# Fused feed-forward, scan and feed-forward kernel: the normalised rows become f16 operands by DMA transposes instead of TensorE f32 transposes

## The chip, the cores and the metric

The kernel runs on one core of a Trainium2 chip. The metric is the device time of one execution in microseconds (us), and the median of the runs counts. Engines are named as in the profile: PE is TensorE, DVE is VectorE, ACT is ScalarE, POOL is GpSimd, SP is SyncE, which here only issues DMAs. "SPq" is SP's queue of DMA issues.

## What is computed

A block of three residual steps on 4096 rows (2 x 2048 tokens) of 1024 channels. The first and the third step are the same routed feed-forward, the second is a selective scan over the tokens.

```
x = x + 0.5 * ffn(layernorm(x), A, B, W, bias)
x = x + scan(layernorm(x), W_xproj, W_dt, b_dt, A_log, D)
x = x + 0.5 * ffn(layernorm(x), A, B, W, bias)

def ffn(x, A, B, W, bias):
    vecs   = einsum('arh,bsh->bsar', A, x)            # 64 experts of rank 16
    routes = top 4 of 64 by norm(vecs), each 1/4
    v      = einsum('bsa,bsar->bsr', routes, vecs)
    delta  = einsum('bsa,ajr,bsr->bsj', routes, B, v)
    return einsum('bsh,jh->bsj', x, W) + bias + delta

def scan(x, ...):
    h = exp(delta * A) * h + delta * B_t * x          # 16 states a channel
    y = sum(h * C_t) ; return y + x * D
```

## The kernel before

Work is cut into 64 units of 128 rows: 32 of the first feed-forward (kind 1) and 32 of the second (kind 2), in an order that `plan` fixes. Units 3 to 60 carry the scan along: its 1024 steps (64 tiles of 16 steps, four groups of four steps a tile) are spread evenly, about 18 a unit. Every engine has a program written out in order, with semaphores between them; nothing is reordered at run time. `scans`, `decays`, `loads` and `states` with two numbers mean "the scan's work between these twentieths of the unit".

In unit *a* the next unit is called *b*. PE does for *a* the product with W (`base`), the scan's small products, the product with B (`routed`), and at the end of the unit already the product of *b* with A (`experts`), each in two halves (nb) of three thirds. The products are f16 in two parts: an operand is a high part plus a low part, `xT[:, 0]` and `xT[:, 1]`, each 128 channels by 128 rows times 8. Thirds 0 and 1 read the high part, third 2 reads the low part. So PE needs the whole of `xT[:, 0]` for *b* at the first of `experts`, and the low part at third 2.

Before the change the operand of *b* is made thus. DVE takes the row statistics (`unit_stats`), ACT works out scale and shift (`prepare`) and writes the normalised rows in f32 to `xn` (`normed`, L842). PE turns them in eight f32 transposes of 128 x 128 into two PSUM banks (`norm_blocks`, L552 with `xn`). ACT copies each bank to `xT[:, 0]` as f16 (`high`, L847), and DVE subtracts that from the bank to give `xT[:, 1]` (`low_part`, L1094). `xn` is used a second time, for the rows that feed the scan (L867), and a third, for its small projections.

SP's order in a unit is: the load of the next rows (L342), the store of the scan's input (L448), two DMA transposes of `uT`, the operand of `routed` (L409), then the scan's loads of twentieths 2 to 9, two small stores (L455, L456), the scan's loads of twentieths 9 to 18, the load of y (L336) and the store of the result (L468). The scan's loads are spreads of 512 KB from scratch memory to all partitions (L361 for POOL's inputs, L354 for ACT's decays), a tile's store (L400) and its second load (L396), and at a new chunk of rows spreads of B and C (L367, L373). POOL's products with B and C are L512, L518 and L528, DVE's scan is L1157, ACT's decays are L942.

Of the kernel before, what the change touches and what calls it, by code (L numbers as in the profile page):

```python
# [119 lines left out]
def build(nc, x, AT, BT, WT, bias, WxT, WdtT, b_dt, A_log, D_par, out):  # L120
# [41 lines left out]
    with ctx:  # L162
# [43 lines left out]
        pjs = xn[:, 0:NX]  # L206
        drs = auxs[:, 0:P]
# [55 lines left out]
        s_xT = sem("s_xT"); s_xhi = sem("s_xhi"); s_xlo = sem("s_xlo")  # L263
        s_vec = sem("s_vec"); s_sq = sem("s_sq"); s_n2 = sem("s_n2"); s_mk = sem("s_mk"); s_gm = sem("s_gm")
# [38 lines left out]
        def _(sp):  # L303
# [106 lines left out]

            def loads(a, lo, hi):
# [28 lines left out]
            def unit(l, a, b):  # L440
# [22 lines left out]
                loads(a, 9, 18)  # L463
# [83 lines left out]
        def _(pe):  # L547
# [20 lines left out]
            def norm_blocks(b, half):  # L568
                if half == 0:
                    pe.wait_ge(s_xn, b.u + 1)  # L570
                if half == 0:
                    pe.wait_ge(s_u, b.u * 2)
                blocks(ptn[half], lambda k: xn[:, (half * KB + k) * P:(half * KB + k + 1) * P], s_xT, idf[:, :])
# [32 lines left out]
            def first_base(a):  # L606
# [10 lines left out]
                for k in range(KD):  # L617
                    pe.wait_ge(s_loW, k + 1)
                    for nb in range(2):
                        nc.tensor.matmul(po[:, nb, :], xT[:, 0, k, :], wW[:, 1, k, nb * HF:(nb + 1) * HF],  # L620
                                         start=False, stop=False)

            def experts(b, nb, third):
                if nb == 0 and third != 1:
                    pe.wait_ge(s_xhi, b.u * 2 + 2)
                    pe.wait_ge(s_xlo, b.u * 2 + (1 if third == 0 else 2))
                last = product(pv[:, nb, :], xT, wA, nb, third, True, True)
                if third == 2:
                    last.then_inc(s_vec, 1)

            def base(a, nb, third):
# [7 lines left out]
                product(po[:, nb, :], xT, wW, nb, third, False, False)  # L639
# [92 lines left out]
            def unit(l, a, b):  # L732
# [61 lines left out]
            norm_blocks(US[0], 0)  # L794
            norm_blocks(US[0], 1)
# [5 lines left out]
        def _(act):  # L801
# [37 lines left out]
            def normed(b, nT):  # L839
# [5 lines left out]
            def high(b, half):  # L845
                act.wait_ge(s_xT, b.u * 2 + 1 + half)
                nc.scalar.activation(xT[:, 0, half * KB:(half + 1) * KB, :].rearrange("p k t -> p (k t)"), ptn[half],  # L847
                                     ACT.Copy).then_inc(s_xhi, 1)
# [16 lines left out]
            def normed2(a, xT_done):  # L865
                act.wait_ge(s_xT, xT_done)
# [78 lines left out]
            def unit(l, a, b):  # L945
# [37 lines left out]
                if b:  # L983
                    normed(b, 2 * (a.f1s - (a.kind == 1)))
                decays(10, 12)
                if b:
                    high(b, 0)
                if b:
                    high(b, 1)
# [15 lines left out]
                if a.kind == 1:  # L1005
                    normed2(a, a.u * 2 + 4)
# [4 lines left out]
            normed(US[0], 0)  # L1011
            high(US[0], 0)
            high(US[0], 1)
# [15 lines left out]
        def _(dve):  # L1029
# [52 lines left out]
            def unit_stats(b):  # L1082
# [4 lines left out]
                dve.wait_ge(s_xn, b.u)  # L1087
                stats("ln1", xin[:, b.p, :], s_mv)

            def low_part(b, half):  # L1090
                dve.wait_ge(s_xhi, b.u * 2 + 1 + half)
                hi = xT[:, 0, half * KB:(half + 1) * KB, :].rearrange("p k t -> p (k t)")
                lo = xT[:, 1, half * KB:(half + 1) * KB, :].rearrange("p k t -> p (k t)")
                V.tensor_tensor(lo, ptn[half], hi, ALU.subtract).then_inc(s_xlo, 1)  # L1094

# [156 lines left out]
            low_part(US[0], 0)  # L1252
            low_part(US[0], 1)
# [56 lines left out]
```

## Time and profile before

| what | value |
|---|---|
| median of 3 runs | 2722.13 us (2721.1 to 2724.64) |
| profiled execution | 2721.68 us, span 2719.8 us |
| PE busy | 2593.5 us, 95% of the span |
| POOL busy | 2350.0 us, 86% |
| DVE busy | 2227.7 us, 82% |
| ACT busy | 1505.0 us, 55% |
| DMA engines | q1, the queue of SP's issues, 43.8% of 16 engines |
| granted PE clock | 0.987 of full speed |

The span is what the profile covers of the execution; 1.9 us lie around it. POOL has nothing to do in the scan's absence, at the start and at the end, so its share is that of a stretch and not of the whole.

### The profile page before, as it was taken

The page shows a single profiled execution, that of the slowest core. Times are in us where ns is not written, and L with a number is a line of the kernel's source. Part 1 is how long each engine was busy: PE and PEld are TensorE (multiplying, and loading weights), DVE is VectorE, ACT ScalarE, POOL GpSimd, SP SyncE. Part 2 cuts the span into 40 slices and gives each one's busy share as a digit, 9 for nine tenths or more (in the row PEclk, how much of TensorE's full clock was granted, in tenths as well). Part 3 has the DMA queues.
Part 4 walks back from the last instruction along what each step waited for, and adds up shares of the span by engine and source line. Part 5 has one row for each costly group of instructions (what it writes and reads, how often), then busy time and mean ns, then how long its engine had stood idle before and what let it go on. Part 6 is the DMA issues. An engine that isn't in the chain of part 4 may idle for free.

```text
span 2719.8 us, 39965 instructions
## 1 busy us (share of the span) xinstructions
PE 2593.5 (95%) x13664; PEld 1178.2 (43%) x13664; DVE 2227.7 (82%) x2933; ACT 1505.0 (55%) x3363; POOL 2350.0 (86%) x703
## 2 busy tenths in 40 slices
PE   4989999999989999999999999999999999999999
PEld 1444444444434444444444444444444444444444
DVE  8448888888878898888888988888888889989943
ACT  5347666665545555555556555555555555656521
POOL 2138998899999999999998999999999999999910
PEclk8989999999999999999999999999999999999999
DMA  5145444644464454645454455544555455554321
GB/s 223 52 117 154 144 148 135 172 141 144 131 183 150 136 156 130 190 141 147 139 177 139 147 153 156 157 130 147 156 172 149 134 156 161 159 144 150 103 63 54
DMA packets 333217, 390.29 MB, mean 143 GB/s; under 512 B 149459, under 2 KB 249939, under 8 KB 333014
## 3 DMA queue, kind: packets, MB, share of 16 engines
q1 hardware_dynamic: 316118, 354.18, 43.8%
q10 hardware_dynamic: 16896, 33.56, 4.0%
q8 instruction: 108, 1.77, 0.3%
q14 instruction: 95, 0.78, 0.1%
HBM read 250.82 MB, written 103.29 MB: 130 GB/s over the span
## 4 chain that ended last, share of the span: by engine, by line
PE 57%; DVE 16%; POOL 6%; DMA 6%; issue 5%; ACT 4%; DVEq 4%; ACTq 1%; SPq 0%; POOLq 0%
PE po L560 20%; PE pv L560 9%; PE po L564 9%; DVE mreg L1157 7%; PE py L727 6%; PE pv L564 4%; POOL mreg L518 3%; PE pv L689 2%; POOL mreg L528 2%; DMA delta_scratch<-mreg 2%; DVE sel L1114 2%; PE pv L708 1%; PE pv L552 1%; DVEq L1116 1%; DMA uT<-sel 1%
## 5 line engine op out<-in xcount | busy, mean ns | idle before, releaser
L528 POOL TENSOR_TENSOR mreg<-mreg 128x2048 f32<-128x2048 f32 x256 | 1163.0, 4543 | 70.7 <-ACT hst L928 70.0
L1157 DVE TENSOR_TENSOR_SCAN mreg<-pA,hst,mreg 128x512 f32<-128x512 f32 (+1 forms) x1024 | 1048.9, 1065 | 50.2 <-ACT pA L942 43.8
L942 ACT ACTIVATE pA<-mreg,nA 128x512 f32<-128x512 f32 (+1 forms) x1280 | 744.4, 598 | 410.0 <-DVE mreg L1157 379.4
L518 POOL TENSOR_TENSOR mreg<-mreg 128x1024 f32<-128x1024 f32 x340 | 796.4, 2370 | 118.3 <-DMA mreg<-delta_scratch 103.8
L560 PE MATMUL po<-wB,uT 128*128 128x512 f16 x2016 | 471.0, 382 | 12.1 <-DVE xin L1080 7.5
L560 PE MATMUL po<-wW,xT 128*128 128x512 f16 x2016 | 474.5, 382 | 0.0
L560 PE MATMUL pv<-wA,xT 128*128 128x512 f16 x2016 | 461.1, 381 | 8.3 <-ACT mreg L911 7.2
L512 POOL TENSOR_TENSOR mreg<-mreg 128x2048 f32<-128x2048 f32 x86 | 390.2, 4537 | 4.0 <-issue 3.8
L560 PEld LDWEIGHTS pv<-wA,xT 128*128 128x128 f16 x2016 | 191.5, 98 | 284.5 <-issue 51.7
L560 PEld LDWEIGHTS po<-wB,uT 128*128 128x128 f16 x2016 | 193.4, 98 | 266.0 <-issue 48.3
L560 PEld LDWEIGHTS po<-wW,xT 128*128 128x128 f16 x2016 | 196.4, 99 | 250.2 <-issue 40.6
L727 PE MATMUL py<-mreg,Em 128*32 128x512 f32 (+1 forms) x2560 | 273.9, 518 | 6.3 <-DVE mreg L1168 6.1
L1157 DVE TENSOR_TENSOR_SCAN mreg<-pA,cst,mreg 128x256 f32<-128x256 f32 (+1 forms) x256 | 244.0, 997 | 15.7 <-ACT pA L942 14.1
L564 PE MATMUL po<-wB,uT 128*128 128x512 f16 x1008 | 238.4, 379 | 0.0
L564 PE MATMUL po<-wW,xT 128*128 128x512 f16 x1008 | 238.4, 379 | 0.0
L564 PE MATMUL pv<-wA,xT 128*128 128x512 f16 x1008 | 238.3, 379 | 0.0
L1098 DVE TENSOR_REDUCE n<-sel 128x32 f32<-128x512 f32 x128 | 87.5, 684 | 172.5 <-ACT sel L855 172.2
L1130 DVE SCALAR_TENSOR_TENSOR xin<-po,sc,xin 128x512 f32<-128x512 f32 x128 | 94.1, 735 | 85.6 <-PE po L564 82.0
L564 PEld LDWEIGHTS po<-wW,xT 128*128 128x128 f16 x1008 | 96.3, 98 | 132.8 <-issue 20.5
L564 PEld LDWEIGHTS pv<-wA,xT 128*128 128x128 f16 x1008 | 97.5, 98 | 125.7 <-issue 10.0
L564 PEld LDWEIGHTS po<-wB,uT 128*128 128x128 f16 x1008 | 96.2, 98 | 122.9 <-issue 21.3
L1071 DVE BATCH_NORM_STATS2 ln_st<-xin 128x6 f32<-128x512 f32 x192 | 122.7, 681 | 9.2 <-DMA xin<-x 3.0
(132 smaller groups left out, 2357.6 us busy)
## 6 DMA issues: line engine op xcount, KB each, us to landing
mreg<-delta_scratch SPq DMA_DIRECT2D x256, 512.0 KB, 5.1
mreg<-xnT_scratch SPq DMA_DIRECT2D x128, 256.0 KB, 5.2
delta_scratch<-mreg ACTq DMA_DIRECT2D x128, 256.0 KB
xin<-x SPq DMA_DIRECT2D x32, 512.0 KB, 4.7
x_scratch<-xin SPq DMA_DIRECT2D x32, 512.0 KB, 4.7
xnT_scratch<-auxs SPq DMA_DIRECT2D x32, 512.0 KB, 3.2
yT_scratch<-mreg SPq DMA_DIRECT2D x64, 256.0 KB, 4.9
uT<-yT_scratch SPq DMA_DIRECT2D x32, 512.0 KB, 6.1
```

Of the source, the lines that this page charges most:

```text
L512: pool.tensor_tensor(h, u, b.broadcast_to([P, 4 * c.parts, c.width]), ALU.mult).then_inc(s_bm, 2)
L518: pool.tensor_tensor(h[:, half * n:half * n + n, :], u, b.broadcast_to([P, n, c.width]), ALU.mult).then_inc(s_bm, 1)
L528: pool.tensor_tensor(h, h, by_c, ALU.mult).then_inc(s_cm, 1)
L560: last = nc.tensor.matmul(dst, lhs[:, 0, k, :], w[:, wb, k, nb * HF:(nb + 1) * HF], start=(first and k == 0 and wb == 0), stop=False)
L564: last = nc.tensor.matmul(dst, lhs[:, 1, k, :], w[:, 0, k, nb * HF:(nb + 1) * HF], start=False, stop=(stop and k == KD - 1))
L689: last = nc.tensor.matmul(pj[:, 0:NX], auxs3[:, k, :], wx[:, k, :], start=(k == 0), stop=(k == KD - 1))
L727: last = nc.tensor.matmul(split(py[32 * s:32 * s + 32, :], c)[:, n, :], Em[:, :], h[:, c.parts * s + n, :], start=(g == 0 and n == 0), sto ...
L942: last = nc.scalar.activation(dst[:, part, :], src[:, part, :], ACT.Exp, scale=nA[:, m:m + 1])
L1071: V.bn_stats(t["st"][:, 6 * n:6 * n + 6], src[:, n * HF:(n + 1) * HF])
L1098: V.tensor_reduce(n2[:, nb * NE // 2:(nb + 1) * NE // 2], sel3[:, nb * NE // 2:(nb + 1) * NE // 2, :], AX.X, ALU.add)
L1130: V.scalar_tensor_tensor(dst, po[:, nb, :], sc[:, 3:4], dst, ALU.mult, ALU.add).then_inc(s_res, 1)
L1157: last = V.tensor_tensor_scan(h, split(pA[:, i % 2, :], c)[:, part, :], h, before, ALU.mult, ALU.add)
```

## The change

The transposes of the normalised rows go from PE to the DMA engines, for units 1 to 63 (unit 0 keeps the old way).

- ACT writes the rows at once as f16 in row form (`high_rows`, into the first half of `xn`'s memory, now called `xr`), in the place of the f32 write. A step later it writes the same rows in f32 to the two PSUM banks (`full_rows`, 512 channels each), in the place of the two copies, one step of `decays` earlier.
- DVE subtracts the f16 rows from the banks and writes the low part in row form (`low_part`), in its old place.
- SP issues two DMA transposes of 256 KB each (`turn_rows`): that of the high part between the two small stores and the loads of twentieth 9, that of the low part between the loads of twentieths 9 to 11 and those from 11 on. The first waits for `high_rows` (and for `base` to be done with the old operand), the second for both halves of `low_part`.
- PE loses `norm_blocks` and waits at `experts` for the landing of these two instead.
- The statistics, and the second small step of a tile on DVE (`delta` at position 1), stay where they are.

```diff
+            def turn_rows(b, part):
+                if part == 0:
+                    sp.wait_ge(s_bs, b.u)
+                    sp.wait_ge(s_xhi, b.u + 2)
+                else:
+                    sp.wait_ge(s_xlo, b.u * 2 + 2)
+                sp.dma_start_transpose(xT[:, part, :, :], xr[:, part, :]).then_inc(s_xc[part], 16)
...
-                loads(a, 9, 18)
+                if b:
+                    turn_rows(b, 0)
+                loads(a, 9, 11)
+                if b:
+                    turn_rows(b, 1)
+                loads(a, 11, 18)
...
             def experts(b, nb, third):
                 if nb == 0 and third != 1:
-                    pe.wait_ge(s_xhi, b.u * 2 + 2)
-                    pe.wait_ge(s_xlo, b.u * 2 + (1 if third == 0 else 2))
+                    pe.wait_ge(s_xc[third // 2], 16 * b.u)
+                    pe.wait_ge(s_xlo, b.u * 2 + 1)
...
                 routed(a, 1, 1)
-                if b:
-                    norm_blocks(b, 0)
-                if b:
-                    norm_blocks(b, 1)
                 states(a, 10)
...
+            def high_rows(b, nT):
                 act.wait_ge(s_nT, nT)
                 act.wait_ge(s_pq, nT // 2)
-                nc.scalar.activation(xn[:, :], xin[:, b.p, :], ACT.Identity, scale=lnb["ln1"]["r"][:, :],
-                                     bias=lnb["ln1"]["nm"][:, :]).then_inc(s_xn, 1)
+                act.wait_ge(s_xc[0], 16 * (b.u - 1))
+                act.wait_ge(s_xc[1], 16 * (b.u - 1))
+                nc.scalar.activation(xr[:, 0, :], xin[:, b.p, :], ACT.Identity, scale=lnb["ln1"]["r"][:, :],
+                                     bias=lnb["ln1"]["nm"][:, :]).then_inc(s_xhi, 1)
+            def full_rows(b, half):
+                act.wait_ge(s_u, b.u * 2)
+                nc.scalar.activation(ptn[half], xin[:, b.p, half * HF:(half + 1) * HF], ACT.Identity,
+                                     scale=lnb["ln1"]["r"][:, :], bias=lnb["ln1"]["nm"][:, :]).then_inc(s_xn, 1)
...
             def low_part(b, half):
+                dve.wait_ge(s_xn, b.u * 2 + 1 + half)
+                dve.wait_ge(s_xhi, b.u + 2)
+                dve.wait_ge(s_xc[1], 16 * (b.u - 1))
+                cols = slice(half * HF, (half + 1) * HF)
+                V.tensor_tensor(xr[:, 1, cols], ptn[half], xr[:, 0, cols], ALU.subtract).then_inc(s_xlo, 1)
```

On SP, in unit 37 of the kernel before, the scan's loads stand around the two small stores (L455, L456) like this; L361 and L354 are spreads, L400 a tile's store.

```order
L361 DMA mreg<-delta_scratch 128x1x1024 [waits s_bm,s_std] x2
L400 DMA yT_scratch<-mreg 128x4x128 [waits s_y]
L354 DMA mreg<-delta_scratch 128x1x1024 [waits s_dA,s_std]
L455 DMA delta_rank_scratch<-auxs 128x128 [waits s_pc]
L456 DMA bc_scratch<-auxs 32x128
L354 DMA mreg<-delta_scratch 128x1x1024 [waits s_dA,s_std]
L396 DMA mreg<-xnT_scratch 128x4x128 [waits s_sty]
```

The same place of the change (its line numbers are some lines on: L363 is the old L361, L356 the old L354, L402 the old L400).

```order
L363 DMA mreg<-delta_scratch 128x1x1024 [waits s_bm,s_std] x2
L402 DMA yT_scratch<-mreg 128x4x128 [waits s_y]
L356 DMA mreg<-delta_scratch 128x1x1024 [waits s_dA,s_std]
L465 DMA delta_rank_scratch<-auxs 128x128 [waits s_pc]
L466 DMA bc_scratch<-auxs 32x128
L419 DMA_TRANSPOSE xT<-xn 128x8x128 [waits s_xhi,s_bs]
L419 DMA_TRANSPOSE xT<-xn 128x8x128 [waits s_xlo]
L356 DMA mreg<-delta_scratch 128x1x1024 [waits s_dA,s_std]
L398 DMA mreg<-xnT_scratch 128x4x128 [waits s_sty]
```

Nothing of the old order moved; two transposes with waits of their own stand in front of the second spread of decays. In other units zero to four of the scan's loads stand between the two.

On PE, in the same unit, before the change, from the middle of `routed` to `experts`:

```order
L560 MATMUL po<-wB,uT 128x512 x16
L552 MATMUL pv<-idf,xn 128x128 [waits s_u,s_xn]
L552 MATMUL pv<-idf,xn 128x128 x3
L552 MATMUL pt<-idf,xn 128x128 x4
L564 MATMUL po<-wB,uT 128x512 x8
L727 MATMUL py<-mreg,Em 32x512 [waits s_cm]
L727 MATMUL py<-mreg,Em 32x512 x3
L560 MATMUL pv<-wA,xT 128x512 [waits s_xlo,s_xhi]
L560 MATMUL pv<-wA,xT 128x512 x15
L564 MATMUL pv<-wA,xT 128x512 [waits s_xlo,s_xhi]
```

And in the change (L575 is the old L560, L579 the old L564, L743 the old L727):

```order
L575 MATMUL po<-wB,uT 128x512 x16
L579 MATMUL po<-wB,uT 128x512 x8
L743 MATMUL py<-mreg,Em 32x512 [waits s_cm]
L743 MATMUL py<-mreg,Em 32x512 x3
L575 MATMUL pv<-wA,xT 128x512 [waits s_xlo,s_xc0]
L575 MATMUL pv<-wA,xT 128x512 x15
L579 MATMUL pv<-wA,xT 128x512 [waits s_xlo,s_xc1]
```

The eight transposes are gone, and the two waits at `experts` are now for landings (`s_xc0`, `s_xc1`) instead of for ACT and DVE.

## Rows read from the trace of the kernel before

**Rows 1.** Page, part 1: busy us (share of the span) xinstructions.

```profile
PE 2593.5 (95%) x13664; PEld 1178.2 (43%) x13664; DVE 2227.7 (82%) x2933; ACT 1505.0 (55%) x3363; POOL 2350.0 (86%) x703
```

**Rows 2.** Windows: length, busy us by engine, PE clock, DMA share, GB/s.

```profile
253.00:2533.00 2280.00, 2214.04 (x11746) 997.96 (x11745) 1969.40 (x2531) 1331.48 (x2970) 2204.34 (x647) 0.99 0.51 150
...
1530.00:1730.00 200.00, 196.97 (x1019) 87.82 (x1016) 176.39 (x210) 116.28 (x245) 199.22 (x61) 1.00 0.52 152
430.00:530.00 100.00, 93.20 (x539) 43.91 (x532) 83.79 (x128) 62.38 (x152) 89.24 (x27) 0.97 0.58 163
```

**Rows 3.** Timeline of PE, end of unit 29: start us, us, line, tiles.

```profile
1318.55 0.60 PE L552 MATMUL pv<-idf,xn 128*128 128x128 f32 x4
1318.99 0.60 PE L552 MATMUL pt<-idf,xn 128*128 128x128 f32 x4
1319.42 1.89 PE L564 MATMUL po<-wB,uT 128*128 128x512 f16 x8
...
1322.24 3.63 PE L560 MATMUL pv<-wA,xT 128*128 128x512 f16 x16
1325.71 1.89 PE L564 MATMUL pv<-wA,xT 128*128 128x512 f16 x8
```

**Rows 4.** Timeline of ACT, same stretch.

```profile
1316.37 1.22 ACT L842 ACTIVATE xn<-xin,ln_nm,ln_r 128x1024 f32<-128x1024 f32 x1
...
1319.68 0.59 ACT L847 ACTIVATE xT<-pt 128x512 f16<-128x512 f32 x1
```

**Rows 5.** Timeline of DVE, same stretch.

```profile
1319.82 0.69 DVE L1094 TENSOR_TENSOR xT<-pv,xT 128x512 f16<-128x512 f32 x1 [0.23 <-ACT xT L847]
1320.43 1.27 DVE L1157 TENSOR_TENSOR_SCAN mreg<-pA,hst,mreg 128x512 f32<-128x512 f32 x1
1321.62 0.67 DVE L1094 TENSOR_TENSOR xT<-pt,xT 128x512 f16<-128x512 f32 x1
```

**Rows 6.** Line L409, all: issue ns min/median/max, then its landing times.

```profile
L409 SPq DMA_TRANSPOSE uT<-sel x128: 1231/1274/4571, 65.5 to 2702.8; - x128
...
DMA to landing us min/median/max: 3.0/3.2/8.1
```

**Rows 7.** DMA issues landing late, window 1088 to 1094: KB, us to landing.

```profile
xin<-x SPq DMA_DIRECT2D x1, 512.0 KB, 8.7
xnT_scratch<-auxs SPq DMA_DIRECT2D x1, 512.0 KB, 9.3
...
uT<-sel SPq DMA_TRANSPOSE x1, 8.1
```

**Rows 8.** Timeline of SP's issues in the same stretch.

```profile
1090.78 0.74 SPq L448 DMA_DIRECT2D xnT_scratch<-auxs  x1
1092.89 7.02 SPq L409 DMA_TRANSPOSE uT<-sel  x2
```

**Rows 9.** Timeline of SP, unit 37.

```profile
1648.82 0.52 SPq L354 DMA_DIRECT2D mreg<-delta_scratch  x1
1649.39 1.32 SPq L455 DMA_DIRECT2D delta_rank_scratch<-auxs  x1
1650.76 1.73 SPq L456 DMA_DIRECT2D bc_scratch<-auxs  x1
1658.29 0.52 SPq L354 DMA_DIRECT2D mreg<-delta_scratch  x1
```

**Rows 10.** Landings of the first L354 and of L456 above, window of each.

```profile
DMA to landing us min/median/max: 10.9/10.9/10.9
...
DMA to landing us min/median/max: 10.2/10.2/10.2
```

**Rows 11.** Timelines of ACT and PE, unit 37.

```profile
1652.86 1.23 ACT L842 ACTIVATE xn<-xin,ln_nm,ln_r 128x1024 f32<-128x1024 f32 x1
...
1659.51 3.63 PE L560 MATMUL pv<-wA,xT 128*128 128x512 f16 x16
```

**Rows 12.** Unit 2: SP's last spread, its landing, PE's first product.

```profile
155.43 0.71 SPq L373 DMA_DIRECT2D mreg<-bc_scratch  x1
...
DMA to landing us min/median/max: 9.1/9.1/9.1
...
157.72 3.62 PE L560 MATMUL pv<-wA,xT 128*128 128x512 f16 x16
```

**Rows 13.** Windows around a pause of PE, columns as in Rows 2.

```profile
448.00:451.00 3.00, 0.75 (x6) 0.42 (x4) 2.96 (x4) 2.25 (x7) 3.00 (x2) 1.00 0.36 109
451.00:454.30 3.30, 3.23 (x6) 1.23 (x7) 3.00 (x5) 1.20 (x3) 3.30 (x2) 0.51 0.65 145
```

**Rows 14.** Window around two L409 transposes, columns as in Rows 2.

```profile
1182.10:1185.50 3.40, 3.40 (x21) 1.17 (x19) 3.40 (x4) 1.75 (x4) 3.26 (x2) 1.00 0.81 154
```

**Rows 15.** Timeline of SP, unit 50: two spreads merged into one row.

```profile
2192.59 16.59 SPq L361 DMA_DIRECT2D mreg<-delta_scratch  x2
2209.23 0.59 SPq L400 DMA_DIRECT2D yT_scratch<-mreg  x1
```

**Rows 16.** Waits, whole span: total us, times, longest.

```profile
DVE xT L1094 <- ACT xT L847: 66.3, 49, 4.9
```

More of the change, by code:

```diff
@@ L263, in build @@
         s_xT = sem("s_xT"); s_xhi = sem("s_xhi"); s_xlo = sem("s_xlo")
+        s_xc = [sem(f"s_xc{n}") for n in range(2)]; s_bs = sem("s_bs")
         s_vec = sem("s_vec"); s_sq = sem("s_sq"); s_n2 = sem("s_n2"); s_mk = sem("s_mk"); s_gm = sem("s_gm")
@@ L638, in base @@
                     nc.tensor.matmul(po[:, nb, :], onesb[:, :], brow[:, nb * HF:(nb + 1) * HF], start=True, stop=False)
-                product(po[:, nb, :], xT, wW, nb, third, False, False)
+                last = product(po[:, nb, :], xT, wW, nb, third, False, False)
+                if (nb, third) == (1, 2):
+                    last.then_inc(s_bs, 1)
             def first_routed(a):
@@ L837, in prepare, with first_normed, first_high @@
                 refine("ln1", 1)
-            def normed(b, nT):
+            def first_normed(b):
+                nc.scalar.activation(xn[:, :], xin[:, b.p, :], ACT.Identity, scale=lnb["ln1"]["r"][:, :],
+                                     bias=lnb["ln1"]["nm"][:, :]).then_inc(s_xn, 2)
+            def first_high(half):
+                act.wait_ge(s_xT, 1 + half)
+                nc.scalar.activation(xT[:, 0, half * KB:(half + 1) * KB, :].rearrange("p k t -> p (k t)"), ptn[half],
+                                     ACT.Copy).then_inc(s_xhi, 1)
+            def high_rows(b, nT):
                 act.wait_ge(s_nT, nT)
                 act.wait_ge(s_pq, nT // 2)
-                nc.scalar.activation(xn[:, :], xin[:, b.p, :], ACT.Identity, scale=lnb["ln1"]["r"][:, :],
-                                     bias=lnb["ln1"]["nm"][:, :]).then_inc(s_xn, 1)
[L845 to L848, printed above, removed]
+                act.wait_ge(s_xc[0], 16 * (b.u - 1))
[6 more added lines that the diff above has]
+                                     scale=lnb["ln1"]["r"][:, :], bias=lnb["ln1"]["nm"][:, :]).then_inc(s_xn, 1)
             def squares(b, nb):
@@ L983, in unit @@
                 if b:
-                    normed(b, 2 * (a.f1s - (a.kind == 1)))
-                decays(10, 12)
+                    high_rows(b, 2 * (a.f1s - (a.kind == 1)))
+                decays(10, 11)
                 if b:
-                    high(b, 0)
+                    full_rows(b, 0)
                 if b:
-                    high(b, 1)
+                    full_rows(b, 1)
+                decays(11, 12)
                 magnitudes(a, 1)
@@ L1010, in _ @@
             prepare(US[0])
-            normed(US[0], 0)
-            high(US[0], 0)
-            high(US[0], 1)
+            first_normed(US[0])
+            first_high(0)
+            first_high(1)
             act.wait_ge(s_scl, 1)
```

34 lines of the change are left out of this document (18 added, 16 removed).

## The prediction

> **What bounds the kernel now.** I read the page first: PE is busy 95% of the span and POOL 86% [rows 1]. Since POOL works only in the scan, I then asked for windows. In the 2280 us from 253 to 2533 PE is busy 2214 us and POOL 2204 us, so PE has 66 us idle there and POOL 76 [rows 2]. In the 200 us from 1530 on both are full, PE 197.0 us and POOL 199.2; around 430 to 530 both have holes [rows 2]. So two engines bound the kernel side by side. Work taken from PE alone shortens it at most until POOL is full, and a wait put on PE costs nearly its length, because PE has 0.6 us (3 us over 4.8 units from 1530) to 1.2 us (66 us over 54 units) to spare in a unit of 42.2 us (2280 us over 54 units).
>
> Next, the place of the change, at the end of unit 29. The eight transposes hold PE from 1318.55 to 1319.42 [rows 3], and PE asks for the high operand at 1322.24 and for the low one at 1325.71 [rows 3]. ACT has the normalised rows ready at 1317.59 (1316.37 + 1.22) [rows 4], and DVE ends the low part at 1322.29 (1321.62 + 0.67) [rows 5]. So today the high operand exists 2 us, and the low one 3.4 us, before PE wants it.
>
> **What goes.** PE loses 1319.42 − 1318.55 = 0.87 us a unit [rows 3], in 63 units 54.8 us. (Each row's own 0.60 us overlaps the next; the starts count.) ACT's work is the same in kind and size: one 1024-wide write and two 512-wide ones. DVE's subtraction keeps its size, and its wait for ACT (66.3 us in 49 cases [rows 16]) mostly goes, since the PSUM banks no longer wait for PE. That makes the low part earlier by up to 1.3 us where it waited, and by 0.2 us in unit 29 [rows 5]. DVE is no bound, so I count it only there.
>
> **What comes, undisturbed.** An existing transpose of this very size is issued in 1.27 us and lands 3.2 us (median) after its issue starts, at least 3.0 [rows 6]. High part in unit 29: 1317.6 + 3.2 = 1320.8, wanted at 1322.24 − 0.87 = 1321.4: covered by 0.6 us. Low part: 1322.1 + 3.2 = 1325.3, wanted at 1325.71 − 0.87 = 1324.8: PE waits 0.5 us. So even the undisturbed case has no cover left. I laid these two sums over all 63 units. The high part alone is in time nearly everywhere; the low part is 0.1 to 0.8 us late in about a third of the units, and in time where ACT's wait used to hold it up.
>
> **What comes, behind other transfers.** This decides. The same transposes take up to 8.1 us [rows 6]. At 1090.78 a 512 KB store was issued that landed 9.3 us later, at 1100.1; the transpose issued at 1092.89 landed 8.1 us later, at 1101.0 [rows 7, 8]. In all 128 cases of L409 the landing is about the larger of 3.1 us and "1.1 us after the last earlier issue of SP has landed". The Trainium skill (DMA: Bandwidth & Descriptors, section Queues, rings and completion order) says that each engine takes descriptors in the order of its ring; the rows above agree.
>
> The old transposes of uT stand in a quiet place. The new ones stand among the spreads. Unit 37: a spread issued at 1648.82 lands 10.9 us later, at 1659.7, and the small store of 1650.76 at 1661.0 [rows 9, 10]. Rows are ready at 1654.1 (1652.86 + 1.23) [rows 11]; the high transpose, behind both, lands near 1661 to 1662, while PE wants it at 1659.51 − 0.87 = 1658.6 [rows 11]: 2.3 to 3.5 us of wait. By this rule, unit for unit:
> - units 2 and 3, the first spreads. In unit 2 the last of eight is issued at 155.43 and lands 9.1 us later, at 164.5; plus 1.1 gives 165.6 against 157.72 − 0.87 = 156.9 [rows 12]: 8.8 us. Unit 3 likewise 6.8 us. Together 15.6 us. Unit 0, without cover, 1.8 us.
> - 16 further units wait 1.1 to 4.3 us for the high part (unit 37 counts with 3.4), together 38 us.
> - the low part adds 15 us over some 20 units (0.1 to 2.6 us). If a store and a spread issued between the two transposes take as long as the slowest rows show, it is 56 us instead.
>
> Waits 15.6 + 1.8 + 38 + 15 = 71 us, less 54.8: PE's path grows by 16 us.
>
> **Two additions.** First, gains and losses don't offset fully: where POOL is full (the 1530 window), a unit without a wait can't be shorter, while a wait still lengthens its unit. About half of the 0.87 us in some 12 such units is lost: 5 us. Second, PE's clock: PE was busy 0.75 us of the 3.0 before 451, and the granted clock in the next 3.3 us was 0.51 (1.2 GHz instead of 2.4) [rows 13]; such a stretch costs about 1.7 us of full-speed work. Eight new waits are over 2 us; I count half of them followed by one: 6 us. The sum is 2721.7 (the profiled execution's own time) + 16 + 5 + 6 = 2749; that execution is 0.4 us below the median. I take 2745, a little lower, since waits on PE let the scan's engines run ahead and some waits then meet an already earlier `high_rows`.
>
> **Costed at nothing.** DMA work: two transposes hold 0.81 of the engines for 3.4 us [rows 14], so two more a unit add 2.8 us in 42, at a DMA share of 0.51 [rows 2]. It is covered by free DMA time; uncovered it shows as later spreads. SP's queue: the second transpose waits for DVE, and behind it stand the spreads of twentieths 11 on. In unit 50 the first L361 goes out at 2192.59 and would now go at about 2207.4; but its partner goes only shortly before 2209.2 anyway [rows 15], when POOL frees the buffer, so the pair as a whole is ready as before. In unit 37 the spread of 1658.29 [rows 9] would go at about 1659.7, behind a transpose that can be issued at 1658.4. By the same reckoning something behind is held by 2 to 5 us in some 25 units; whether it is wanted that soon, no row shows. If that slack fails, ACT's decays and POOL's products wait; that is rival 3.
>
> **Rivals.**
> 1. *The transposes are hidden.* If waits on PE only eat slack that the removal itself makes, and the queue rule is softer next to these loads, PE saves 30 to 55 us, and POOL's 76 idle us [rows 2] let most of it through: 2670 to 2710, say 2693. For it: the high part has cover in two thirds of the units. Against it: unit 37's sum, and full POOL rows. The Trainium skill (DMA: Bandwidth & Descriptors, section Rules for kernel authors) says that a DMA's fixed cost overlaps if it is issued early and waited for late; here the rows show that it can't be issued early, as its input is ready only 4.65 us before use in unit 29 (1317.59 to 1322.24 [rows 3, 4]). It decides if the waits on PE stay under 0.5 us a unit. Chance 0.24.
> 2. *Nothing to measure.* Waits of 55 us equal the saving, or POOL keeps its pace through both: 2717 to 2727. Chance 0.13.
> 3. *The spreads come late too.* Each held by 2 to 5 us in 25 units, with 1 to 2 us of it passed on to POOL and ACT, plus the 56 us case for the low part: 2745 + 25 + 25, some 2795. Chance 0.13.
> 4. *My forecast*, PE waits for landings: 2728 to 2785, likeliest 2745. Chance 0.50.
>
> The change does what it says on PE in any case; the order of its instructions shows the eight transposes gone.
>
> **How the numbers follow.** Faster than 2716.7 (over 0.2%, about what a measurement of this kernel can tell) is rival 1 and a bit: 0.25. Within 0.2%: 0.14. Slower: 0.61. The range takes off a tenth at each end: low 2690, where half of rival 1 is left out, high 2790, the end of the forecast with the larger price for the low part. The forecast's own range is 2728 to 2785.
>
> **What would show it.** L552 on `xn` falls to the scan's share, about 55 us of PE's time. Waits "PE pv <- DMA xT<-xn" should appear, 50 to 90 us in all, long in units 2 and 3 and then in phases (units 20, 28 to 31, 36 to 39, 44 to 47, 52 to 54) in which spreads stand near. Landings of xT should have a median near 4 us with a tail to 9. DVE's wait for ACT before the low part should be gone. I am wrong if the DMA wait on PE is under 30 us, or if it is there but POOL's busy share in 253 to 2533 rises.

## The result and the profile after

| | before | after |
|---|---|---|
| median | 2721.61 us (4 runs, 2720.61 to 2724.64) | 2744.94 us (4 runs, 2742.18 to 2751.87) |
| profiled execution | 2721.68 us, span 2719.8 | 2742.18 us, span 2740.4 |
| granted PE clock, profiled execution | 0.987 | 0.986 (0.980 to 0.986 over the four) |

The kernel before took 2720.84 to 2723.83 us (medians) beside the experiments below. One execution of `e9_mixed`, at 6786 us, was disturbed; it stands in no ratio, and the median of the other nine is 2719.22 us.

The ratio is 1.0089, 95% interval 1.0077 to 1.0102: slower by 0.9%, against 2745.0 us predicted. The page of the kernel after, part 1, the line that answers to [rows 1]:

```profile
PE 2551.3 (93%) x13160; PEld 1120.8 (41%) x13160; DVE 2228.1 (81%) x2933; ACT 1525.9 (56%) x3363; POOL 2349.1 (86%) x703
```

PE has 504 instructions and 42.2 us less to do (2593.5 − 2551.3), yet the span is 20.6 us longer. So its idle time grew by 62.8 us, from 126.3 to 189.1 (span less busy). The windows of [rows 2], of the kernel after, same columns:

```profile
253.00:2533.00 2280.00, 2160.79 (x11225) 941.40 (x11227) 1952.74 (x2505) 1343.27 (x2954) 2184.32 (x643) 0.99 0.61 162
1530.00:1730.00 200.00, 188.26 (x949) 79.70 (x948) 171.85 (x203) 114.74 (x243) 194.16 (x57) 1.00 0.62 160
430.00:530.00 100.00, 94.10 (x551) 43.87 (x550) 84.29 (x132) 68.13 (x171) 89.50 (x26) 0.98 0.60 161
```

POOL, busy 2204 of 2280 us before, is busy 2184 now: POOL has the same work (2349.1 us in all against 2350.0), spread over a longer time. In the stretch from 1530, where both were full, PE has 11.7 us idle and POOL 5.8. What ended PE's idle time (the waits: total us, times, longest):

```profile
PE pv L575 <- DMA xT<-xn: 83.5, 44, 8.5
PE pv L724 <- DVE sel L1146: 20.1, 22, 2.8
PE pv L579 <- DMA xT<-xn: 10.2, 12, 2.6
```

These are 93.7 us of waits for the two transposes: 83.5 for the high part, 10.2 for the low one. Before, these two products waited 1 us for their operand. As PE's idle time grew by only 62.8, some 30 us of its other waits have gone; L724's, for one, was 26.3 before. Landings of the new transposes, all 126 (the line's duration in ns is that of the issue):

```profile
L419 SPq DMA_TRANSPOSE xT<-xn x126: 1231/1242/5454, 85.6 to 2701.8; - x126
...
DMA to landing us min/median/max: 3.0/4.1/9.5
```

The median is 0.9 us over that of uT's transposes [rows 6]. Unit 37, the example of the prediction; SP's issues and PE's first product with A:

```profile
1665.44 0.74 SPq L466 DMA_DIRECT2D bc_scratch<-auxs  x1
1670.33 5.78 SPq L419 DMA_TRANSPOSE xT<-xn  x2
...
1676.82 3.41 PE L575 MATMUL pv<-wA,xT 128*128 128x512 f16 x15 [1.94 <-DMA xT<-xn]
```

The high transpose landed 6.5 us after its issue and PE waited 1.94 us; 2.3 to 3.5 was forecast. The first spread ahead of it landed in 4.2 us here instead of 10.9 [rows 10], before the transpose was issued; of SP's transfers only the small store of 1665.44 was still under way. ACT had issued its two stores at 1664.84 and 1665.40.

### The profile page after: what moved, and what is told of

Read it like the earlier page. It is cut to its first block, busy times and chain, and to the rows that moved or that the text cites. A ratio compares the mean times of both kernels' runs of the same rounds, so it can differ in the third digit from the quotient of the medians.

```text
span 2740.4 us, 39303 instructions
## 1 busy us (share of the span) xinstructions
PE 2551.3 (93%) x13160; PEld 1120.8 (41%) x13160; DVE 2228.1 (81%) x2933; ACT 1525.9 (56%) x3363; POOL 2349.1 (86%) x703
## 4 chain that ended last, share of the span: by engine, by line
PE 43%; DVE 18%; DMA 12%; ACT 10%; issue 6%; DVEq 5%; ACTq 2%; POOL 2%; SPq 1%; POOLq 0%
PE po L575 12%; PE pv L575 12%; DMA xT<-xn 7%; DVE mreg L1189 7%; PE pv L579 6%; PE po L579 5%; PE py L743 3%; PE pv L705 2%; ACT pA L966 2%; DMA delta_scratch<-mreg 2%; ACT xn L865 2%; DVE sel L1146 2%; DVEq L1148 1%; DVE pv L1149 1%; PE pv L724 1%
## 5 line engine op out<-in xcount | busy, mean ns | idle before, releaser
L543 POOL TENSOR_TENSOR mreg<-mreg 128x2048 f32<-128x2048 f32 x256 | 1161.0, 4535 | 74.6 <-ACT hst L952 74.5
L575 PE MATMUL pv<-wA,xT 128*128 128x512 f16 x2016 | 478.6, 392 | 88.5 <-DMA xT<-xn 83.5
L575 PE MATMUL po<-wB,uT 128*128 128x512 f16 x2016 | 470.0, 381 | 5.4 <-DMA uT<-sel 2.9
L575 PE MATMUL po<-wW,xT 128*128 128x512 f16 x2016 | 473.4, 382 | 0.0
L575 PEld LDWEIGHTS pv<-wA,xT 128*128 128x128 f16 x2016 | 194.8, 100 | 383.5 <-DMA xT<-xn 121.1
L575 PEld LDWEIGHTS po<-wB,uT 128*128 128x128 f16 x2016 | 193.3, 98 | 257.9 <-issue 45.2
L575 PEld LDWEIGHTS po<-wW,xT 128*128 128x128 f16 x2016 | 195.8, 98 | 247.7 <-issue 36.6
L743 PE MATMUL py<-mreg,Em 128*32 128x512 f32 (+1 forms) x2560 | 273.2, 517 | 7.0 <-DVE mreg L1200 7.0
L579 PE MATMUL pv<-wA,xT 128*128 128x512 f16 x1008 | 238.4, 380 | 10.2 <-DMA xT<-xn 10.2
L579 PE MATMUL po<-wB,uT 128*128 128x512 f16 x1008 | 238.5, 380 | 0.0
L579 PE MATMUL po<-wW,xT 128*128 128x512 f16 x1008 | 238.4, 380 | 0.0
L878 ACT ACTIVATE sel<-pv 128x512 f32<-128x512 f32 x128 | 75.7, 592 | 172.6 <-PE pv L579 168.9
L579 PEld LDWEIGHTS pv<-wA,xT 128*128 128x128 f16 x1008 | 96.3, 98 | 139.1 <-DMA xT<-xn 17.7
L579 PEld LDWEIGHTS po<-wB,uT 128*128 128x128 f16 x1008 | 96.3, 98 | 133.4 <-issue 21.3
L579 PEld LDWEIGHTS po<-wW,xT 128*128 128x128 f16 x1008 | 96.4, 98 | 132.8 <-issue 20.5
```

The lines of the kernel that those rows point to most:

```text
L543: pool.tensor_tensor(h, h, by_c, ALU.mult).then_inc(s_cm, 1)
L575: last = nc.tensor.matmul(dst, lhs[:, 0, k, :], w[:, wb, k, nb * HF:(nb + 1) * HF], start=(first and k == 0 and wb == 0), stop=False)
L579: last = nc.tensor.matmul(dst, lhs[:, 1, k, :], w[:, 0, k, nb * HF:(nb + 1) * HF], start=False, stop=(stop and k == KD - 1))
L743: last = nc.tensor.matmul(split(py[32 * s:32 * s + 32, :], c)[:, n, :], Em[:, :], h[:, c.parts * s + n, :], start=(g == 0 and n == 0), sto ...
L878: nc.scalar.activation(sel[:, nb * HF:(nb + 1) * HF], pv[:, nb, :], ACT.Square).then_inc(s_sq, 1)
```

## Experiments

All times are medians, each beside runs of the kernel before on the same chip; each "ratio" is against those, with its 95% interval. Waits and landings are those of one profiled execution.

### What the change could give at most, and what its transfers cost others

```diff
-                if b:
-                    turn_rows(b, 0)
-                loads(a, 9, 11)
-                if b:
-                    turn_rows(b, 1)
-                loads(a, 11, 18)
+                loads(a, 9, 18)
...
-                nc.scalar.activation(xr[:, 0, :], xin[:, b.p, :], ACT.Identity, scale=lnb["ln1"]["r"][:, :],
+                nc.scalar.activation(xT[:, 0, :, :].rearrange("p k t -> p (k t)"), xin[:, b.p, :], ACT.Identity, scale=lnb["ln1"]["r"][:, :],
```

This is e1; the low part goes straight to `xT[:, 1]` likewise. e2 is e1 with both calls of `turn_rows` back in their places, now transposing from `xT` into `xr`, which nobody reads. In both, the operand of units 1 to 63 is not turned, PE waits for ACT and DVE instead of for landings, and ACT rather than SP waits for `base` to be done with the old operand; everything else is as in the change.

> The changed kernel without its 126 DMA transposes: ACT and DVE write the row form straight into the operand, and PE waits for them alone. Left out is the transposing, so the products are of rows that were not turned. Theory W (the cost is PE's wait for the landings; PE and POOL bound the kernel side by side): the 94 us of waits go, PE keeps the 55 us saved, POOL lets most of it through: 2690 us, 2678 to 2705. Rival P (PE's 55 us were never worth anything, POOL is the bound): 2715 us or more.

> As the run without transposes, but with the same two 256 KB DMA transposes a unit in the same places of SP's queue with the same waits, into memory that nobody reads; PE does not wait for them. The operand is again not turned. Theory W: the traffic and the hold on SP's queue cost little, 0 to 8 us over the run without transposes, about 2695 us, and DMA waits on PE are under 5 us. Rival S (the spreads of the scan come late behind the held queue, and that is the loss): within 8 us of the changed kernel, 2737 us or more, with longer waits of ACT and POOL for spreads.

Measured: e1 2704.19 us, ratio 0.993 (0.9912 to 0.9947); e2 2704.57 us, 0.9936 (0.9915 to 0.9958). Windows from 253 to 2533 and from 1530 to 1730 of e1, and then from 253 to 2533 of e2:

```profile
253.00:2533.00 2280.00, 2181.78 (x11282) 955.04 (x11335) 1971.53 (x2537) 1352.45 (x2974) 2205.94 (x648) 0.99 0.51 150
1530.00:1730.00 200.00, 192.60 (x961) 83.46 (x964) 173.26 (x208) 114.53 (x244) 196.97 (x60) 0.98 0.53 155
```

```profile
253.00:2533.00 2280.00, 2182.89 (x11289) 955.03 (x11348) 1973.23 (x2538) 1353.94 (x2978) 2207.61 (x649) 0.99 0.63 163
```

Two things follow. With all 54.8 us gone from PE and no wait in return, the kernel gains 19 us: PE now has 98 us idle in the stretch, POOL 74, against 66 and 76 before [rows 2]. So two thirds of the saving are lost. What keeps them back is not shown: POOL's idle time hardly moved, and in the 200 us from 1530 POOL is less full than before (197.0 against 199.2), so it is not simply POOL running full; waits of the two engines on each other, by way of ACT and DVE, are the likelier reason. And the same transposes, issued in the same places behind the same waits, cost nothing that these runs can tell (some 5 us either way), as traffic (DMA share 0.63 against 0.51) or as a hold on SP's queue. The 40 us between e2 and the change (2705 to 2745) come with one thing, PE's wait for the landings.

### The start

```diff
+NOLD = 5
...
+                if b and b.u < NOLD:
+                    norm_blocks(b, 0)
+                    norm_blocks(b, 1)
```

> The changed kernel with units 1 to 4 turned the old way, by PE; the change holds from unit 5 on. The trace of the changed kernel is 8.3 us behind the kernel before at the first product of unit 4's next unit. Theory W: 7 to 9 us less than the changed kernel, 2736 to 2738 us. Rival (the start's waits are made up later, since POOL has idle time after them): 0 to 3 us less, 2742 to 2745 us.

Units 1 to 4 keep the f32 transposes on PE. Measured: 2747.12 us (2738.53 to 2753.92), 1.009 (1.0072 to 1.0108), no faster than the change: the rival expectation held. Waits of e3:

```profile
PE pv L578 <- DMA xT<-xn: 62.8, 40, 3.8
...
PE pv L582 <- DMA xT<-xn: 11.5, 15, 2.7
```

The high part's waits fell by 21 us and the time by nothing that can be told. Against the 8.5 us of wait in unit 2 and 6.1 in unit 3 of the change, PE's start of `experts` was 8.3 us later than before at unit 4 (as it was 11.7 at unit 2). So what is lost in the start is partly made up, in stretches where PE is not full. Its long waits, 15.6 us of my sum, bear little on the time.

### Where the high transpose loses its time

Units 7 and 8 have nothing of SP in flight, and still their high transposes landed late. Timelines of unit 8 of the change, ACT's issues of its two delta stores, SP's transpose and PE's first product, and then the transpose's landing:

```profile
432.12 0.53 ACTq L944 DMA_DIRECT2D delta_scratch<-mreg  x1
432.68 0.53 ACTq L944 DMA_DIRECT2D delta_scratch<-mreg  x1
...
437.84 1.25 SPq L419 DMA_TRANSPOSE xT<-xn  x1
...
442.51 3.63 PE L575 MATMUL pv<-wA,xT 128*128 128x512 f16 x16 [0.34 <-DMA xT<-xn]
```

```profile
DMA to landing us min/median/max: 4.6/4.6/4.6
```

Packets by queue in the window from 437.8 to 441.1, and then in that from 441.1 to 442.4 (packets, MB, share; q1 is SP's queue, q10 ACT's):

```profile
q1 hardware_dynamic: 507, 0.13, 68.2%
q10 hardware_dynamic: 129, 0.25, 19.7%
```

```profile
q1 hardware_dynamic: 549, 0.13, 48.6%
```

Up to 441.1 a quarter of a megabyte of ACT's stores is moved beside the transpose; then ACT's queue is empty, and 1.3 us later the transpose has landed. At 2558.49, after the last tile, no store is near, and it lands in 3.0 us. Over the 63 high transposes only 7 landed within 3.2 us, all in units without a store of ACT; of the low ones, 4 to 5 us later, 34 did. 32 high transposes were issued behind ACT's stores with nothing of SP under way, and they took 3.6 to 6.7 us. My rule counted SP's queue alone, and the trace before could not have told: none of the 128 transposes of `uT` has a store of ACT in the 12 us ahead of it. So I moved the two sides against each other.

```diff
-                loads(a, 2, 9)
+                loads(a, 2, 7)
...
-                loads(a, 9, 11)
+                loads(a, 7, 9)
...
+                if b:
+                    high_rows(b, 2 * (a.f1s - (a.kind == 1)))
                 decays(8, 9)
                 delta_out(a, 0)
-                if b:
-                    prepare(b)
-                decays(9, 10)
-                if b:
-                    high_rows(b, 2 * (a.f1s - (a.kind == 1)))
-                decays(10, 11)
```

This is e4: statistics, rows, low part and both transposes two twentieths earlier, on SP, ACT and DVE alike; the stores stay. The next is e5, the change with the stores behind the high transpose (in units with one tile only):

```diff
                 decays(8, 9)
-                delta_out(a, 0)
+                if 1 in a.zs:
+                    delta_out(a, 0)
...
-                decays(12, 16)
+                decays(12, 14)
+                if 1 not in a.zs:
+                    delta_out(a, 0)
+                decays(14, 16)
```

e6 is e4 with the stores after `decays(12, 13)` (again in units with one tile only), which is behind both of its transposes.

> The changed kernel with the statistics, the scale and shift, the rows, the low part and both transposes about two twentieths of a unit (some 4 us) earlier, the small second step of a tile left where it is. Theory W: the high rows are ready some 8 us before use instead of 4.7, PE's waits for landings fall from 94 us to under 25, and the time comes near the run without transposes: 2700 us, 2685 to 2715. Rival S (the held queue of SP is the loss): 2730 us or more, since the hold is the same or longer.

> The changed kernel with ACT's two stores of a tile's deltas (256 KB each, on ACT's own DMA queue) issued some 6 us after the rows instead of 5.5 us before them, except in the 9 units with two tiles. In the changed kernel's trace a high transpose lands in 3.04 us where no packet of ACT's queue is in flight, and in 3.8 to 7.3 us, 1.3 us after the last such packet, where one is. Theory A (ACT's stores hold the high transposes up): their landing falls to about 3.1 us where SP has nothing ahead, PE's waits for landings fall from 94 us to 35 to 60, and the time to 2715 to 2732. Theory Q (only SP's own earlier transfers count, as I predicted): waits stay over 80 us and the time within 5 us of 2745.

> The version with statistics, rows, low part and transposes two twentieths earlier, which took 2915 us, with ACT's two stores moved behind both transposes (again not in the 9 units with two tiles). In that version the stores went out 1 us before the high transpose, which landed after 8.0 us at the median. Theory A: with the stores out of the way PE's waits for landings fall from 185 us to under 40 and the time from 2915 to 2700 to 2730. Rival (the early statistics and rows themselves starve the scan, ACT and DVE waiting on each other): waits for landings fall but the time stays over 2780.

Measured: e4 2915.24 us, 1.0706 (1.0685 to 1.0726); e5 3082.28 us, 1.1322 (1.1301 to 1.1342); e6 2827.99 us, 1.0396 (1.0376 to 1.0415). Near 1710 us in e4, and near 1538 us in e5:

```profile
1710.50 1.08 ACTq L944 DMA_DIRECT2D delta_scratch<-mreg  x2
1711.67 1.81 SPq L419 DMA_TRANSPOSE xT<-xn  x1
1721.55 2.79 PE L575 MATMUL pv<-wA,xT 128*128 128x512 f16 x8 [3.11 <-DMA xT<-xn]
```

```profile
1538.04 0.54 ACTq L944 DMA_DIRECT2D delta_scratch<-mreg  x1
1538.60 0.53 ACTq L944 DMA_DIRECT2D delta_scratch<-mreg  x1
1538.52 1.34 SPq L419 DMA_TRANSPOSE xT<-xn  x1
...
1549.96 2.32 PE L579 MATMUL pv<-wA,xT 128*128 128x512 f16 x5 [7.24 <-DMA xT<-xn]
```

I had moved the high transpose of e4 onto the stores (1.2 us behind them instead of 5.7), and the stores of e5 onto the low transpose. A transpose that starts beside the stores lands about 10 us later. PE's waits for the part that was hit, e4's high one and e5's low one:

```profile
PE pv L575 <- DMA xT<-xn: 178.8, 57, 8.5
```

```profile
PE pv L579 <- DMA xT<-xn: 328.5, 48, 10.2
```

The landings of the 63 high and the 63 low transposes apart, taken one by one from the traces:

| kernel | high: median us | within 3.2 us | low: median us |
|---|---|---|---|
| the change | 4.9 | 7 | 3.1 |
| e4 | 9.8 | 7 | 6.6 |
| e5 | 3.1 | 46 | 10.1 |
| e6 | 3.1 | 48 | 3.1 |

The times that I had expected of e4 and e5 were wrong by 200 us and more, but the collision moved just as the stores did. Their times grew by more than their waits for landings (185 us in all in e4, 351 in e5). Part of the rest is PE's clock, which was granted at 0.962 and 0.936 over the two spans: the low product with A in the change and in e5, the same matmuls (part 5 of the pages):

```profile
L579 PE MATMUL pv<-wA,xT 128*128 128x512 f16 x1008 | 238.4, 380 | 10.2 <-DMA xT<-xn 10.2
```

```profile
L579 PE MATMUL pv<-wA,xT 128*128 128x512 f16 x1008 | 315.2, 470 | 328.7 <-DMA xT<-xn 328.5
```

e6 has hardly any collision: median 3.1, and PE's wait for the high part falls to 33.0 us. It is slow all the same, for other reasons. Its waits:

```profile
DVE mreg L1191 <- ACT pA L966: 169.1, 66, 5.2
POOL mreg L543 <- ACT hst L952: 153.4, 69, 5.6
SPq L363 <- DMA delta_scratch<-mreg: 130.7, 29, 9.3
```

In the change the first two are 74.5 us each and the third, a wait of SP's queue, is 23.9. DVE's wait for the decays comes with the early rows: it is 192.8 us in e4 and 72.3 in e5. ACT also waits longer for the statistics (151.8 us against 108.8), and the decays stand behind that wait and the row writes in ACT's order; which of the two counts more is not told apart. The third wait comes with the late stores (113.5 us in e5): the scan's loads need what the stores write. So the place of the rows was no slack to spend, and the stores could not simply go later either.

### SP's loads behind the transpose

```diff
-                loads(a, 2, 9)
+                loads(a, 2, 6)
...
                 if b:
                     turn_rows(b, 0)
-                loads(a, 9, 11)
+                loads(a, 6, 11)
```

> The changed kernel with SP's loads of twentieths 6 to 9 behind the high transpose instead of ahead of it, so that hardly a spread or tile store stands before it in SP's queue; ACT's stores unchanged. Theory Q: the units with SP transfers in flight at the issue, which hold some 55 of the 94 us of waits, lose most of it; waits 45 to 55 us, time 2728 to 2735. Theory A: ACT's stores hold the transpose in the same units anyway, so waits stay at 75 us or more and the time within 6 us of 2745, or above it if the spreads now come late.

Measured: 2780.05 us, 1.0212 (1.0196 to 1.0228). Waits of e7:

```profile
ACT pA L966 <- DMA mreg<-delta_scratch: 79.7, 25, 6.1
...
PE pv L579 <- DMA xT<-xn: 70.7, 40, 6.0
PE pv L575 <- DMA xT<-xn: 34.5, 35, 8.3
```

The high part's waits fall from 83.5 to 34.5 us, but the low transpose now stands behind the loads (10.2 to 70.7 us), and the decays wait 79.7 us for spreads that come late, against 5.5. So SP's own queue does delay the transposes too, and its loads can't stand back. For the high part it counts less than ACT's stores: the 63 landings add up to 319 us in the change and 279 in e7, where 63 undisturbed ones would be 192. All in all waits change places, and the kernel loses another 35 us.

### The stores made small, with a control

```diff
+                t = min(t, 1)
...
+                    wide = CT if t < 2 else 64
-                    dst = dd_d[(2 * t + n) * P:(2 * t + n + 1) * P, :].rearrange("(i s) c -> s i c", s=4)
-                    act.dma_start(dst, dd[:, n, :]).then_inc(s_std, 16)
+                    dst = dd_d[(2 * t + n) * P:(2 * t + n + 1) * P, 0:wide].rearrange("(i s) c -> s i c", s=4)
+                    act.dma_start(dst, dd[:, n, 0:wide]).then_inc(s_std, 16)
```

e8 is the change with this edit, e11 the kernel before with it. Both leave out seven eighths of what ACT stores, from the third tile on, and the spreads read the first two tiles' data.

> The changed kernel with ACT's two delta stores cut from 256 KB to 32 KB each (for all tiles but the first two); the spreads then all read the data of the first tiles, so the scan's inputs are wrong values of the right size, and everything is issued in the same places. Theory A (the high transpose lands about 1.3 us after the last packet of ACT's stores): the small stores are done before the transposes are issued, so landings of xT have a median of 3.1 to 3.5 us instead of 4.1, stay long only where SP's own spreads are in flight, and the waits of PE for them fall from 94 us to 40 to 60. By the exchange seen so far (94 us of waits against 40 us of time over the kernel without transposes) the time is 2718 to 2732, say 2726. Theory B (SP's own queue alone delays them, ACT's stores are a coincidence of place): median stays near 4, waits 80 to 95, time 2738 to 2748. If the spreads of 512 KB gain by the lower traffic too, POOL's waits fall and the time can go down to 2715.

> The control for the small stores: the kernel before with ACT's two delta stores cut from 256 KB to 32 KB each (all tiles but the first two; the spreads all read the data of the first tiles, so the scan's inputs have wrong values). Theory A (the stores cost the change its time through the landings of xT, which this kernel does not have): 2714 to 2723, say 2719, so that the small stores give the kernel before at most a quarter of the 36 us that they gave the change. Rival T (smaller stores free ACT and POOL from waits whatever turns the rows): the kernel before gains 15 us or more, below 2707, and the 36 us say little on the landings.

Measured: e8 2708.61 us, 0.9952 (0.9937 to 0.9967), so 36 us under the change; e11 2718.68 us, 0.9978 (0.997 to 0.9987), some 5 us under the kernel before. In the same unit 8 of e8, SP's issue, the packets by queue until 434.9, and the landing:

```profile
431.80 1.25 SPq L420 DMA_TRANSPOSE xT<-xn  x1
```

```profile
q1 hardware_dynamic: 1056, 0.26, 44.0%
```

```profile
DMA to landing us min/median/max: 3.1/3.1/3.1
```

ACT issued its stores 5.7 us ahead, as before, but they are done, and the transpose lands in 3.1 us instead of 4.6. Over the kernel (waits and landings of e8):

```profile
PE pv L580 <- DMA xT<-xn: 30.6, 29, 4.1
PE pv L576 <- DMA xT<-xn: 24.4, 11, 8.1
```

```profile
DMA to landing us min/median/max: 3.0/3.1/8.9
```

Of the high part's 83.5 us of waits 24.4 are left, 19 of them in units 0, 2 and 3. 49 of 63 high transposes land within 3.2 us, and the 63 landings add up to 210 us (319 in the change). The low part's waits rise to 30.6 since PE asks 1 to 2 us sooner. With the places unchanged and only the stores made small, this shows that ACT's stores hold the high transposes up; the control takes about 5 of the 36 us away from it. The time came out 9 us under the low end of the 2718 to 2732 us that I had expected. Whether the spreads gained by the lower traffic next to the transposes isn't told apart.

### Turning only where it pays

```diff
+                if b and b.u in OLD:
+                    norm_blocks(b, 0)
+                    norm_blocks(b, 1)
```

The units in `OLD` are turned on PE, as before the change: in e9 the 27 before which PE had waited over 1.5 us, in e10 every second one, in e12 eleven more than in e9.

> The changed kernel, but the rows of 27 units (those before which PE waited over 1.5 us in the trace of the change: 1, 3 to 7, 13, 15, 16, 21, 29 to 31, 36 to 41, 45, 46, 48, 52 to 56) are turned on PE as before. Theory W (each wait costs its place): PE has 27 x 0.87 = 23.5 us of transposes again and loses about 78 of its 94 us of waits; with POOL as the floor of 2704 us seen without any transposes, the time is 2708 to 2722, say 2715, below the kernel before. Rival M (waits are where PE and the scan's engines settle against each other; take them from one place and they come up in another, as in the start's units): waits in the other 36 units grow, 40 us or more remain, time 2728 to 2745.

> The changed kernel, but the rows of every second unit (2, 4, ... 62) are turned on PE as before, with no regard to the waits. Half of the saving and half of the waits: 2730 to 2737 if places are independent, which is also what no choice of places would give. It is the control for the run with the chosen 27 units: if that one is not at least 8 us faster than this one, the choice of places is worth nothing.

> The mixed kernel with 38 units turned on PE instead of 27: those before which PE waited over 0.87 us in the trace of the mixed one (8, 14, 18, 22, 23, 25, 32, 34, 43, 44, 47) are added. Theory W: 11 more transposes cost 9.6 us and take away about 17 us of waits: 2708 to 2718, say 2714, faster than the kernel before by 0.1 to 0.5%. Rival M (waits come up elsewhere as they did from the first mixed kernel): 2717 to 2724, no difference from the mixed one or from before.

Measured: e10 2732.62 us, 1.004 (1.0025 to 1.0055), halfway as expected. e9 2719.37 us, 0.9989 (0.9978 to 1.0), 13 us faster than e10, so the choice of units is worth something. e12 2719.99 us, 0.9992 (0.9983 to 1.0002), no better than e9. Waits of e9 and then of e12:

```profile
PE pv L592 <- DMA xT<-xn: 19.6, 18, 3.4
PE pv L596 <- DMA xT<-xn: 3.6, 7, 1.9
```

```profile
PE pv L592 <- DMA xT<-xn: 4.0, 8, 2.1
PE pv L596 <- DMA xT<-xn: 2.9, 7, 0.8
```

Few waits are left, and still there is next to no gain; e9 lies in the range of its first expectation, above the 2715 us named as likeliest, and e12 in that of its rival. e9's window fits this: both engines are full once more there.

```profile
1530.00:1730.00 200.00, 198.12 (x1010) 86.38 (x1014) 176.22 (x211) 117.75 (x252) 198.90 (x60) 1.00 0.52 153
```

### What a microsecond on PE is worth

All kernels with the rows in their old place, by the net change of PE's path: 0.87 us for each unit turned by DMA, less the waits for landings.

| kernel | units by DMA | saved | waits | net | time against before | by the ratio's 95% interval |
|---|---|---|---|---|---|---|
| the change | 63 | 54.8 | 93.7 | −38.9 | +23.3 | +21 to +28 |
| e3 | 59 | 51.3 | 74.3 | −23.0 | +23.9 | +20 to +29 |
| e10 | 32 | 27.8 | 46.4 | −18.6 | +10.3 | +7 to +15 |
| e9 | 36 | 31.3 | 23.2 | +8.1 | −2.9 | −6 to 0 |
| e12 | 25 | 21.8 | 6.9 | +14.9 | −3.8 | −5 to +1 |
| e1 | 63 | 54.8 | 0 | +54.8 | −19.1 | −24 to −14 |

By the medians, a microsecond lost on PE costs 0.55 to 0.6 in the change and e10 (1.0 in e3, whose profiled execution was 8.6 us under its median); one gained brings 0.35 in e1. e9 and e12 gave 0.36 and 0.25, but their gains are hardly clear of nothing. So these are rough prices; that a gain brings less than a loss costs is plain only from e1 beside the change. e8 falls out of this line (55.0 us of waits, net −0.2, but −8.5 after its control).

## Why the prediction was right, point by point

- **What bounds it.** Right in that work taken from PE alone brings little, and stronger than I used it: e1 puts a number on the cap, 19 of 54.8 us. That POOL running full is what caps it is not shown (its idle time stayed as it was). The 2693 us of rival 1 were thus out of reach: even with transposes that cost nothing it is 2704.
- **What goes, 54.8 us.** The instructions on `xn` fell from 768 to 264, as forecast. PE's busy time fell by 42.2. The missing 12.6 us are for the most part slower PE after the waits. The high product with A, the one that waits, is 17.5 us more busy for the same 2016 matmuls (first two lines below), and in e1, where it waits for no landing, it is not (third line); PE's other products are some 7 us less busy than before. In unit 2 after the wait of 8.5 us (below), PE ran its next 3.3 us at a granted clock of 0.50, 1.2 GHz, so the same work counts as more busy time.
- **DVE's wait** of 66.3 us before the low part [rows 16] is gone, as I said: 5.2 us now.
- **Undisturbed landing, 3.2 us.** Right as a row (3.04 us in the quiet units at the end), wrong as a forecast for the high part: nearly no unit of the scan is undisturbed.
- **Behind other transfers.** The step that failed is "the landing is about the larger of 3.1 us and 1.1 us after the last earlier issue of SP has landed". It held for uT's transposes because these stand where ACT stores nothing. Here ACT's queue counts as well: 1.3 us after its last packet in unit 8. The Trainium skill (DMA: Bandwidth & Descriptors, section Queues, rings and completion order) states that each engine takes turns between the queues that have work for it, and that a completion is signalled only after that engine's earlier writes, across its queues. The 4.6 us beside 129 packets of ACT's queue against 3.1 us beside none agree with both; no run here tells the two apart.
- **The sum of waits.** 71 predicted (its terms add to 70.4), 93.7 measured. High part outside units 0, 2 and 3: 38 predicted, 64 measured (83.5 − 19.2). With ACT's stores made small only 5.4 of them are left (24.4 − 19.0), so my 38, all laid on SP's queue, was mostly theirs, too. Low part: 15 predicted, 10.2 measured, as PE came later to it. Start: 17.4 against 19.2. The units were the named ones and others, before and between them (4 to 6, 12, 14 and 15 among them).
- **What a wait costs.** "A wait put on PE costs nearly its length" was too much: 0.6 of it in the change. This and the missed stores offset each other. Net −38.9 at full price would be 2760 us; net −16 as predicted, at 0.6, would be 2731. So the hit on the microsecond is partly luck: the direction and the mechanism (PE waits for the landings) held, what delays the landings was only in part what I had said, and two sizes were off in opposite ways.
- **The two additions.** The asymmetry of gains and losses was counted with 5 us; by e1 it is far more, whatever its cause. The clock term of 6 us is too small for the new waits by themselves, which cost 17.5 us, and right as a net: over all of PE's busy time, by the clock's own rows, the slower clock took 25.5 us of full-speed time before and 32.0 in the change. That net is under 17.5 very likely because some 30 us of PE's other waits went. Those are the profiled executions; the change's other three ran at a lower granted clock (0.980 to 0.983), so there the term was larger.
- **Costed at nothing.** DMA traffic and the hold on SP's queue: right, shown by e2, and rival 3 falls with it.
- **Signs.** DMA waits on PE 93.7 us (50 to 90 forecast), a median landing of 4.1 (near 4), a tail to 9.5 (9), long in units 2 and 3, POOL's busy share in the stretch not risen. The first is out of its bounds, the tail a little, the rest within them.

The high product with A before, in the change and in e1 (part 5 of the pages):

```profile
L560 PE MATMUL pv<-wA,xT 128*128 128x512 f16 x2016 | 461.1, 381 | 8.3 <-ACT mreg L911 7.2
```

```profile
L575 PE MATMUL pv<-wA,xT 128*128 128x512 f16 x2016 | 478.6, 392 | 88.5 <-DMA xT<-xn 83.5
```

```profile
L562 PE MATMUL pv<-wA,xT 128*128 128x512 f16 x2016 | 461.9, 381 | 15.2 <-ACT mreg L919 12.7
```

The windows of unit 2's wait and after it:

```profile
163.00:169.00 6.00, 0.00 (x0) 0.00 (x0) 2.89 (x5) 2.43 (x8) 0.00 (x0) 0.58 0.99 141
169.00:172.30 3.30, 2.88 (x7) 1.04 (x8) 0.00 (x0) 1.16 (x4) 0.00 (x0) 0.50 1.02 300
```

## What to carry to other kernels

Before work moves from a compute engine to the DMA engines, ask how long its input exists before its use. Here that was 4.65 us against a landing of 3.0 at best, and 3.6 to 9.4 beside other transfers. Read the landing time from the very place where the transfer will stand, and count all queues that are in flight there, those of other engines' stores too. And measure the ceiling first: one kernel that leaves the new operation out altogether shows what the best case is worth, and here it was a third of the sum saved. Count, too, what the engine does after a wait: here PE's work behind the new waits took 17.5 us longer.

## What the runs showed of the hardware

- A DMA transpose issued on SP's queue 5.7 us behind two 256 KB stores on ACT's queue lands in 4.6 us instead of 3.0 in unit 8, and in 3.6 to 6.7 us in the 32 units where nothing of SP's queue is under way; issued within 1.2 us of them, in about 10 (e4, e5). With the stores cut to 32 KB it is 3.1 again in unit 8, and at the median (e8).
- Two transposes a unit into memory that nobody reads raised the DMA share from 0.51 to 0.63 and left the time unchanged (2704.57 against 2704.19 us).
- A matmul of 128x512 f16 in the high product with A took 381 ns on the mean without waits for landings (e1), 392 in the change and 424 in e4; in e5 the low product's took 470 against 380. The granted clock fell to 0.50, 1.2 GHz, after unit 2's wait.
- The issue of a transpose, 1.24 us alone, took up to 5.45 us in unit 2, where eight spreads were queued ahead of the pair.
